# Moving the gate's small matrices and scale terms from VectorE to GpSimd, and reordering ScalarE's first steps, in a two-layer residual kernel

## The reference, cut to what matters

```python
# layer 0: x (32, 128, 128); u = v = fside (32, 1, 128, 16); b = cond (32, 128)
z1 = einsum('bfi,bir->bfr', x, v) / 128;  z = einsum('bfr,bor->bfo', z1, u) / 16
x = x + gelu(x @ W.T + fc_bias + z + b)                      # exact gelu
# layer 1: four routed experts (two used) and a shared one
gate_in = concat([x.mean(1), hp.mean(1), wp.mean(1)])         # all tokens; head+proprio; wrist+proprio
logits  = gate_in @ gate_w + gate_b
scale, shift = split(silu(cond) @ time_w + time_b)
scores  = softmax(logits * (1 + scale) + shift)               # 4 experts
w_be    = top-2 of scores, renormalised
for e in range(4):
    out += w_be[:, e] * mask[e] * (gelu_tanh(x @ ew1[e] + eb1[e]) @ ew2[e] + eb2[e])
x = x + out + gelu_tanh(x @ sw1 + sb1) @ sw2 + sb2
```

## Time and profile before

| | |
|---|---|
| median of 3 runs | 241.34 us (241.19 to 241.63) |
| the profiled execution's own time | 241.15 us |
| its span, first to last instruction | 238.9 us |
| granted TensorE clock, mean | 0.998 |
| PE busy | 231.5 us (97%) |
| DVE busy | 200.5 us (84%) |
| ACT busy | 142.7 us (60%) |
| POOL busy | 19.4 us (8%) |

### The profile page before, as it was taken

How to read it: one execution, slowest core, us unless ns; L and a number is a source line. 1 busy time by engine, 2 the same in 40 slices (tenths; PEclk the granted TensorE clock), 3 DMA queues, 4 the chain that set the end, 5 groups by cost and what they waited for, 6 DMA issues and landing times.

```text
span 238.9 us, 3425 instructions
## 1 busy us (share of the span) xinstructions
PE 231.5 (97%) x1194; PEld 197.4 (83%) x1194; DVE 200.5 (84%) x456; ACT 142.7 (60%) x279; POOL 19.4 (8%) x46
## 2 busy tenths in 40 slices
PE   8999899999999999999999999999999999999995
PEld 7886587788788887888798887888888889899894
DVE  0389999999896867976899998996999989778883
ACT  3598999816965097743977179443654075553531
POOL 8000000014000020002000030002000030020000
PEclk9999999999999999999999999999999999999999
DMA  6993000000010000100000000100010000100011
GB/s 181 293 287 95 3 0 0 3 0 0 3 44 0 0 0 4 44 0 1 3 33 11 0 3 1 44 0 3 0 44 0 3 0 1 44 3 1 0 44 44
DMA packets 11256, 7.40 MB, mean 31 GB/s; under 512 B 3776, under 2 KB 10600, under 8 KB 11240
## 3 DMA queue, kind: packets, MB, share of 16 engines
q1 hardware_dynamic: 10760, 7.07, 10.0%
q0 software_dynamic: 192, 0.03, 0.2%
q10 hardware_dynamic: 288, 0.10, 0.2%
HBM read 5.09 MB, written 2.10 MB: 30 GB/s over the span
## 4 chain that ended last, share of the span: by engine, by line
PE 75%; ACT 12%; DVE 9%; issue 2%; POOL 0%; DVEq 0%; ACTq 0%; POOLq 0%
PE ps L521 23%; PE ps L523 22%; PE ps L522 22%; ACT h L428 5%; DVE hs_lo L815 2%; PE ps L527 2%; PE ps L539 2%; ACT L428 2%; ACT L409 2%; PE ps L570 1%; ACT W_raw L414 1%; PE ps L664 1%; DVE segsum L790 1%; PE ps L578 1%; ACT hs_hi L443 1%
## 5 line engine op out<-in xcount | busy, mean ns | idle before, releaser
L428 ACT ACTIVATE h<-ps,b_col 128x512 f32<-128x512 f32 (+1 forms) x160 | 90.6, 640 | 58.8 <-PE ps L523 55.5
L833 DVE SCALAR_TENSOR_TENSOR hs_lo<-h,w_be,hs_hi 128x344 fp32r<-128x344 f32 (+1 forms) x124 | 73.5, 654 | 0.0
L521 PE MATMUL ps<-x_hi,W_hi 128*128 128x512 f32 (+2 forms) x168 | 66.0, 393 | 2.7 <-ACT hs_hi L431 1.4
L523 PE MATMUL ps<-x_lo,W_hi 128*128 128x512 f32 (+2 forms) x168 | 60.8, 362 | 0.0
L522 PE MATMUL ps<-x_hi,W_lo 128*128 128x512 f32 (+2 forms) x168 | 60.7, 361 | 0.0
L521 PE MATMUL ps<-hs_hi,W_hi 128*128 128x512 f32 (+1 forms) x156 | 57.2, 367 | 0.4 <-DVE hs_lo L833 0.4
L523 PE MATMUL ps<-hs_lo,W_hi 128*128 128x512 f32 (+1 forms) x156 | 56.9, 365 | 0.0
L522 PE MATMUL ps<-hs_hi,W_lo 128*128 128x512 f32 (+1 forms) x156 | 56.6, 363 | 0.0
L825 DVE TENSOR_SCALAR hs_hi<-h,w_be 128x344 fp32r<-128x344 f32 (+1 forms) x120 | 44.9, 438 | 8.4 <-PE ps L523 4.2
L521 PEld LDWEIGHTS ps<-x_hi,W_hi 128*128 128x128 f32 x168 | 31.7, 189 | 12.1 <-ACT h L428 2.9
L522 PEld LDWEIGHTS ps<-x_hi,W_lo 128*128 128x128 f32 x168 | 31.8, 189 | 4.3 <-issue 1.0
(11 more groups left out here) (121 smaller groups left out, 178.3 us busy)
## 6 DMA issues: line engine op xcount, KB each, us to landing
W_raw<-in_L_cond_ew SPq DMA_DIRECT2D x8, 256.0 KB, 5.7
out<-x_tok SPq DMA_DIRECT2D x7, 256.0 KB, 2.1
x_tok<-in_x SPq DMA_DIRECT2D x3, 512.0 KB, 6.2
x_tok<-in_x SPq DMA_DIRECT2D x2, 256.0 KB, 3.4
W_raw<-in_L_cond_sw SPq DMA_DIRECT2D x2, 256.0 KB, 4.6
out<-x_tok SPq DMA_DIRECT2D x2, 128.0 KB, 1.7
F_pad<-in_fside_Bx1x1024x SPq DMA_DIRECT2D x2, 64.0 KB, 5.6
W_raw<-in_L_cond_W ACTq DMA_DIRECT2D x1, 64.0 KB, 2.9
```

What stands on the lines that cost most here:

```text
L428: ins = nc.scalar.activation(span(h[:, k % 3, c, :], s), up_bank(k, c), ACT.Gelu_apprx_tanh, bias=b1_col[:, s, c:c + 1])
L521: nc.tensor.matmul(dst, w_hi, m_hi, start=start, stop=False)
L523: return nc.tensor.matmul(dst, w_hi, m_lo, start=False, stop=stop)
L833: nc.vector.scalar_tensor_tensor(lo[:, :, c], h[:, k % 3, :, c], w_be[:, t * NB + b, s - 1:s], f32(hi[:, :, c]), ALU.mult, ALU.subtract).t ...
```

## The change

Four edits. On ScalarE, `x1_high(1)` is moved from behind the loop over the front tiles into it, behind the fourth weight of t = 1. On ScalarE, `gate_tanh(0)` is moved from ahead of `gelu(1)` to behind it. `gate_matrices` leaves VectorE, and `gate_mul` and `gate_add` leave `modulation`; both are done by GpSimd, ahead of its wait for the low weights and of the clearing of `fT_block`, so that this clearing now comes behind a wait for `mod_read`. On VectorE, `split(0)` is moved ahead of `read_logits(0)` and `gate_maximum(0)`.

```diff
+            pool.wait_ge(gate_loads_in, 16 * 2)
+            inv = 1.0 / (HEAD + PROP)
+            chained(nc.gpsimd.tensor_scalar(gate_raw[:, 0, :], gate_raw[:, 0, :], 1.0 / L, None, ALU.mult))
+            chained(nc.gpsimd.tensor_scalar(gate_raw[:, 1:3, :], gate_raw[:, 1:3, :], inv, None, ALU.mult))
+            chained(nc.gpsimd.tensor_tensor(gw[:, 0, :], gate_raw[:, 1, :], gate_raw[:, 0, :], ALU.add))
+            nc.gpsimd.tensor_tensor(gw[:, 2, :], gate_raw[:, 2, :], gate_raw[:, 0, :], ALU.add).then_inc(gw_ok, 1)
+            nc.gpsimd.tensor_tensor(gw[:, 1, :], gate_raw[:, 2, :], gw[:, 0, :], ALU.add).then_inc(gw_ok, 1)
+            pool.wait_ge(mod_read, 1)
+            chained(nc.gpsimd.tensor_scalar(gate_mul[:, :, :], mod[:, :, 0:E], 1.0, None, ALU.add))
+            chained(nc.gpsimd.tensor_tensor(gate_add[:, :, :], gate_mul[:, :, :],
+                                            gate_b_row[:, :].unsqueeze(1).to_broadcast([128, B, E]), ALU.mult))
+            nc.gpsimd.tensor_tensor(gate_add[:, :, :], gate_add[:, :, :], mod[:, :, E:2 * E], ALU.add
+                                    ).then_inc(gate_scale_ok, 1)
+
             pool.wait_ge(w_lo_ok, made(2))
             nc.gpsimd.memset(fT_block, 0.0).then_inc(block_zero_ok, 1)
...
                 if t < 2:
                     weight_high(WEIGHTS[t + 2])
-            x1_high(1)
+                if t == 1:
+                    x1_high(1)
             act.wait_ge(b1_ok, 1)
             gelu(0)
+            gelu(1)
             gate_tanh(0)
-            gelu(1)
...
-            def gate_matrices():
-                dve.wait_ge(gate_loads_in, 16 * 2)
-                inv = 1.0 / (HEAD + PROP)
-                chained(nc.vector.tensor_scalar(gw_full[:, :], gate_raw[:, 0, :], 1.0 / L, None, ALU.mult))
-                chained(nc.vector.scalar_tensor_tensor(gw[:, 0, :], gate_raw[:, 1, :], inv, gw_full[:, :],
-                                                       ALU.mult, ALU.add))
-                nc.vector.scalar_tensor_tensor(gw[:, 2, :], gate_raw[:, 2, :], inv, gw_full[:, :], ALU.mult, ALU.add)
-                chained(nc.vector.scalar_tensor_tensor(gw[:, 1, :], gate_raw[:, 2, :], inv, gw[:, 0, :],
-                                                       ALU.mult, ALU.add))
...
                                         ALU.add).then_inc(mod_read, 1)
-                dve.wait_ge(mod_read, 1)
-                chained(nc.vector.tensor_scalar(gate_mul[:, :, :], mod[:, :, 0:E], 1.0, None, ALU.add))
-                chained(nc.vector.tensor_tensor(gate_add[:, :, :], gate_mul[:, :, :],
-                                                gate_b_row[:, :].unsqueeze(1).to_broadcast([128, B, E]), ALU.mult))
-                chained(nc.vector.tensor_tensor(gate_add[:, :, :], gate_add[:, :, :], mod[:, :, E:2 * E], ALU.add))
...
                 dve.wait_ge(segsum_ok, NSEG * (g + 3))
+                if g == 0:
+                    dve.wait_ge(gw_ok, 2)
...
                 dve.wait_ge(logit_ps, g + 1)
+                if g == 0:
+                    dve.wait_ge(gate_scale_ok, 1)
...
                     weight_low(WEIGHTS[2])
-                    gate_matrices()
                     segment_sums(0, 1)
...
             modulation()
+            split(0)
             read_logits(0)
             gate_maximum(0)
-            split(0)
             gate_ranks(0)
```

More of the change, by code:

```diff
@@ L115, in build @@
         gate_add = sb("gate_add", [128, B, E])
-        gw_full = sb("gw_full", [128, E])
         gw = sb("gw", [128, NSEG, E])
@@ L178, in build @@
             sem("tanh_g_ok"), sem("w_ok"), sem("bias2_ok"), sem("x1b_ok"))
+        gw_ok, gate_scale_ok = sem("gw_ok"), sem("gate_scale_ok")
         shared_hi_ok, act_hi_ok = sem("shared_hi_ok"), sem("act_hi_ok")
```

## The result

The changed kernel takes 242.20 us in the median of 7 runs (241.52 to 242.32), the kernel before 241.19 in 7 runs on the same chip (240.5 to 241.63). The ratio is 1.0035 with a 95% interval of 1.0020 to 1.0050: slower, by 0.85 us by the ratio (the two medians are 1.01 apart). The forecast was 241.6, which it counted as the same within 0.48 us; the time lies on the upper edge of its range (241.0 to 242.2), and by its own bound of 0.48 the kernel is slower. A second measurement of the same kernel on another chip (`e9_after_again`) gave 1.0036 [1.0020, 1.0053].

The account below looks back on a forecast made before the run. TensorE, busy 231.5 of 238.9 us, was taken as the bound, its nearly gapless run starting behind VectorE's `w_be`. The exchange (-0.04) plus one GpSimd meeting (+0.28) gave +0.24 on 241.34: 241.6 us, range 241.0 to 242.2.

Parts of the forecast that it names:

- rival (c): VectorE's split from 25.91: three GpSimd operations each meet a VectorE instruction, +0.80 us, 242.1, slower; chance 0.16.
- The sum: On `w_be`, and so on the end: -0.04 plus 0.28 gives +0.24 us, 241.6 on the median, counted as same.
- signs of being wrong: Front: cast starting before 25.5, L926 waiting for GpSimd, or `up(4)` starting more than 0.5 us away from 38.83.
- x1_high(1) earlier: ScalarE's front: it fits a 0.86 us hole, so table load and `gelu(0)` come 0.52 us earlier.
- rival (e): ScalarE's table load stays behind the biases, lead only 0.24 us; +0.52, 241.9, or 241.6 without a meeting; chance 0.06.
- gate_tanh behind gelu(1): ScalarE: 0.59 idle and 0.16 us leave the path of `gelu(1)`; TensorE's `up(2)` ends about 1.2 us earlier.
- Gate matrices: VectorE loses four tiny instructions, about 0.6 us; GpSimd's five end by 19.3, nothing waits, no gain counted.
- Scale and offset for a wait: VectorE behind the modulation: 0.92 us of work removed, 0.88 of waiting for `gelu(0)` added; `w_be` 0.04 earlier.
- rival (d): VectorE's 0.92 us is a true gain because `gelu(0)` is done by 25.1; 240.4, faster; chance 0.15.
- GpSimd beside VectorE: GpSimd's third operation meets VectorE's cast of `split(0)` once, costing 0.28 us over 0.69 alone.
- turns: GpSimd beside VectorE: both slow at once (0.97 against 0.69, 2.23 against 1.33), looking unlike a full wait.
- rival (b): Exclusive access: VectorE's cast waits out a whole GpSimd operation, up to 0.47 us; +0.43, 241.8; chance 0.13.

Follow-up runs that it names:

- e9_after_again: The changed kernel run once more, unedited, on another chip; ratio 1.0036 to the kernel before, 241.90 us.
- e1_layout: The changed kernel with the removed `gw_full` allocation put back unused, so later tiles lie where they lay before; ratio 1.0005 to the kernel before, 241.40 us.
- e2_fill12: e1_layout with twelve one-element memsets on VectorE early in front; ratio 0.9989 to the kernel before, 240.91 us.
- e4_scale_dve: e1_layout with scale and offset given back to VectorE, right behind the modulation, and eight one-element memsets; ratio 0.9980 to the kernel before, 240.77 us.
- e3_act_only: The kernel before with only the two ScalarE edits; ratio 0.9998 to the kernel before, 241.17 us.
- e6_clear_first: e2_fill12 with GpSimd's clearing of `fT_block` moved ahead of its wait for `mod_read`; ratio 0.9990 to the kernel before, 240.66 us.
- e5_before_shift: The kernel before with `gw_full` moved behind the last tile, no instruction changed, `hs_hi` at 191264; ratio 1.0061 to the kernel before, 242.29 us.
- e12_pool8: The kernel before with eight one-element memsets on GpSimd behind its front DMAs; ratio 0.9964 to the kernel before, 240.44 us.
- e7_best: e4_scale_dve with all four high parts of step 1 made by ScalarE, removing VectorE's cast in `split(1)`; ratio 0.9969 to the kernel before, 240.35 us.
- e11_before_up: The kernel before with 32 more bytes at `gw_full`, no instruction changed, `hs_hi` at 191328; ratio 1.0038 to the kernel before, 242.14 us.
- e10_pad_hs: The changed kernel with 32 empty bytes ahead of `hs_hi` only, returning it to 191296; ratio 1.0009 to the kernel before, 241.54 us.

## Why the prediction was right or wrong

The time came out on the edge of the range, and that was luck: the range held it through the meetings of rival (c), while in the kernel two terms that stood in no case (+0.8 and +0.25) were partly paid back by a third (-0.5). The front's mechanism was mostly right; the sum was not.

The account is: +0.53 on `w_be` (-0.03 exchange, +0.32 meeting, +0.25 stop, -0.01 rest), +0.8 from the 32 bytes, -0.5 outside the span, in sum +0.8, measured +0.85 (0.35% of 241.2; 1.01 by the medians). The forecast's sum was the first two terms, +0.24; they measured +0.29. Leaving terms out one by one agrees: without the shift the account gives about 0 (`e1_layout`, 1.0005), without the stop too 0.03 - 0.25 = -0.22, that is 0.9991 (`e2_fill12`, 0.9989), and without the 0.22 of the meeting too -0.44, that is 0.9982 (`e4_scale_dve`, 0.9980). The intervals of these ratios are 0.3 to 0.45 us to either side, as wide as the smaller terms; these rest on the traces, and the ratios do not contradict them.

**The step that failed** is "The sum": it held nothing for a declaration that goes. The claims that the rest keeps its start distances, and that TensorE is nearly gapless from 44.71 on, so that whatever moves this start moves the end by as much, failed there. TensorE was as gapless as before, but its 512-column down products were 3.4 ns longer each. The start moved to 45.01 and the end by 1.1, where 0.3 would have followed. None of the forecast's signs of being wrong showed this (the cast started at 25.69, L932 did not wait, `up(4)` started at 39.13, 0.30 away), because all of them lie in the front. By the front's steps and the saved time outside the span alone, the result would have been no change.

Point by point:

- *x1_high(1) earlier*: right. The table load started at 20.79 where 21.00 was forecast, with `mod` 0.23 earlier, and the first gelu 1.29 behind it. It did not wait for the biases; rival (e) is out.
- *gate_tanh behind gelu(1)*: right. `up(2)` ended near 29.5 (30.0 forecast, again 0.2 to 0.3 of it the execution's), the 0.73 hole is gone, and TensorE's lead became the 1.13 hole ahead of `down(1)` and a second of 0.56 ahead of `up(4)`. `e3_act_only` shows it worth nothing by itself.
- *Gate matrices*: nothing waited for them, as forecast; GpSimd did them from 10.79 to 12.63. That adding instructions to GpSimd's list could pay outside the span was not foreseen.
- *Scale and offset for a wait*: right. VectorE idles 0.92 where 0.88 was forecast, and the exchange gave 0.03 where 0.04 was forecast. L932 waited for nothing. That is why rival (d), faster, failed: VectorE's removed work ended in a wait for `gelu(0)`. `e4_scale_dve` puts the work back into that wait, and its `w_be` is 0.06 from before.
- *GpSimd beside VectorE*: the size was right, 0.28 forecast and 0.32 read, the place was not. The forecast had it on the cast, some 0.28 over 0.69. The cast lost 0.06, and the first low part 0.26. Read with the two timelines: the cast runs from 25.69 to 26.43, GpSimd's third operation starts at 25.95 but ends only at 26.74, 0.3 behind the cast; meanwhile the low part, which starts at 26.35, takes 1.48 for 1.22. So, as I read the rows, each in turn had to let the other finish a whole instruction; no run shows the two apart from each other. What the runs show is the third operation at 0.79, where the one before it, of the same size, took 0.40, and a clearing of 0.52 that costs nothing: the two low parts take 2.62 with it beside them (`e2_fill12`) and without it (`e6_clear_first`). By these the forecast's "turns" in place of a "full wait" was the wrong choice, though rival (b) put the price of the full wait on the cast, 0.47, and was too high as well.
- *Rival (c)*, slower by three meetings, had the time (242.1) and the side, and not the cause. There was one meeting; the slowness came from elsewhere.
- *The stop* ahead of the second cast, +0.25, is in no case. The order of the list was looked at for what each operation waits for, and not for where it stands.

**What stays open.** Why a start 32 or 96 bytes past a multiple of 128 slows a moving tile against one 64 past isn't shown, only that it does, in both directions and with no other edit. `x1_hi` and `x1_lo` begin on a multiple of 128 in all these kernels (118912 and 135296), and their matmuls are about 232 ns apart, between the two; whether that is their start or their being other products, no run tells. What stops VectorE ahead of the second cast is open too, and so are 0.6 us of `e5_before_shift`. Why more instructions on GpSimd shorten the time outside the span can't be read from a trace that starts later. Of `e12_pool8`'s 0.87 us (0.36% of 241.35), 0.45 lie there; the other 0.4 is in its median span (238.7 against 239.1), and its profiled execution shows no place for it. No kernel with both the eight memsets and the edits of `e7_best` was run.

## What to carry to other kernels

Before costing a diff's instructions, compare the addresses of all tiles behind a declaration that comes or goes: here 32 bytes cost 0.8 us and outweighed every edit of the schedule, and in a kernel bound by TensorE (busy 97% here) the starts of its moving tiles are worth a trial of their own (three were tried here). When VectorE's work is moved away and the time turns into a wait for another engine, leave it where it is: here it was free in the wait (`w_be` within 0.06 us of before, `e4_scale_dve`), and on GpSimd it came back as a meeting of 0.32. A stop whose named releaser was done long ago (here 3.3 us, 29.12 against 32.43) is tested by shifting the list by some tiny instructions (here eight or twelve), and not by looking for a wait.

## What the runs showed of the hardware

- 512-column matmuls whose moving tiles start 32 or 96 bytes past a multiple of 128 (`hs_hi` at 191264 and 191328) started 233.3 to 233.5 ns apart in the mean of three kinds (changed kernel, `e5_before_shift`, `e11_before_up`), against 229.8 to 230.0 with the tiles 64 bytes past one (191296; the kernel before, `e1_layout`, `e10_pad_hs`); over 240 of them that is 0.8 us. Kernels with this shift alone took 1.0061 (`e5_before_shift`) and 1.0038 (`e11_before_up`).
- VectorE stood idle for 0.29 us ahead of the second cast, 0.25 longer from start to start than before, with the tile that the view names finished 3.3 us earlier (29.12 against 32.43 in the changed kernel). It did so in four traces (the changed kernel, `e9_after_again`, `e1_layout`, `e10_pad_hs`), and did not when twelve (`e2_fill12`, `e6_clear_first`) or eight (`e4_scale_dve`) one-element memsets stood ahead in its list.
- Eight memsets of 0.32 us in all on an idle GpSimd came with 0.45 us less outside the span (`e12_pool8`, 1.77 against 2.22).
- An operation of 128x128 on GpSimd took 0.79 us beside VectorE's cast and first low part, where the one before it, of the same size, took 0.40; the two-input VectorE operation behind the cast took 1.48 for 1.22, 0.26 longer (changed kernel against `e4_scale_dve`), and nothing longer for a GpSimd memset of 0.52 (2.62 for two in `e2_fill12` with it and in `e6_clear_first` without).
